# Split key and value weights made in the first attention, query stacks taken from DRAM, three key stages, one row product a unit, values multiplied by single key tiles

## The reference, cut to what matters

```
q = layernorm(x) @ Wq.T + bq ; k = ctx @ Wk.T + bk ; v = ctx @ Wv.T + bv
scores = q . k / sqrt(32)          (L1: clipped to +-50, masked keys at -50)
heads = softmax(scores) @ v ; x = x + tanh(gate) * (heads @ Wo.T + bo)
```

## Time and profile before

| | before |
|---|---|
| median of 3 executions | 3316.87 us |
| the profiled execution, its own time | 3318.72 us |
| its span on the core | 3316.8 us |
| mean granted TensorE clock | 0.894 of 2.4 GHz |
| busy share of the span: TensorE, VectorE, ScalarE, GpSimd | 81%, 57%, 36%, 30% |
| first attention, its blocks | about 0 to 330 us |
| L1 attention, start to the last take | about 545 to 971 us |
| L2 attention | about 1635 to 2090 us |
| L3 attention | about 2380 to 2840 us |

### The profile page before, as it was taken

One profiled execution on the slowest core, in us unless ns is written; L12 is line 12 of the kernel. 1 busy time (PEld: TensorE's weight loads), 2 busy tenths in 40 slices (PEclk: granted clock), 3 DMA queues, 4 the chain that ended last, 5 costly groups with the idle time before them and its releaser, 6 DMA issues. The chain is left out here.

```text
span 3316.8 us, 36567 instructions
## 1 busy us (share of the span) xinstructions
PE 2702.4 (81%) x11319; PEld 1708.5 (52%) x11319; DVE 1898.5 (57%) x3303; ACT 1208.7 (36%) x2586; POOL 984.4 (30%) x438
## 2 busy tenths in 40 slices
PE   7998797787787289999678888748678888789898
PEld 3554686544323156566365553336455553367565
DVE  3453675487665898985647774512347774534321
ACT  2111222355543597874114444211214444212111
POOL 2000000366713011010017776033217776032122
PEclk9988898878888599999788998879888998899999
DMA  9520122232200101010223221073423321021722
GB/s 325 163 75 22 70 76 101 76 111 63 77 1 29 38 14 51 26 51 13 87 61 106 76 52 36 1 255 73 136 62 101 80 54 36 14 92 48 261 55 47
DMA packets 122048, 258.08 MB, mean 78 GB/s; under 512 B 26656, under 2 KB 29729, under 8 KB 118561
## 3 DMA queue, kind: packets, MB, share of 16 engines
q1 hardware_dynamic: 104672, 218.70, 21.1%
q0 software_dynamic: 12864, 29.06, 3.7%
q10 hardware_dynamic: 4352, 8.39, 0.8%
HBM read 155.44 MB, written 47.39 MB: 61 GB/s over the span
## 5 line engine op out<-in xcount | busy, mean ns | idle before, releaser
L1768 POOL TENSOR_TENSOR L_attn_total<-L_attn_total,L_attn_probs 128x2048 f32<-128x2048 f32 x120 | 554.1, 4618 | 145.7 <-ACT L_attn_probs L1707 139.5
L1707 ACT ACTIVATE L_attn_probs<-L_attn_s_ps 128x512 f32<-128x512 f32 x512 | 290.6, 597 | 373.3 <-PE L_attn_s_ps L1588 366.1
L1813 DVE TENSOR_REDUCE L_attn_row_max<-L_attn_rows_ps 128x1 f32<-128x512 f32 x512 | 336.7, 682 | 151.3 <-PE L_attn_rows_ps L1568 146.1
L1588 PE MATMUL L_attn_s_ps<-L_attn_q_stack,L_attn_k_stack 98*128 98x512 f32 (+1 forms) x768 | 334.7, 468 | 106.9 <-ACT L_attn_probs L1707 76.7
L516 PE MATMUL L_ffn_hidden<-L_ffn_x_high,L_ffn_up_high 128*128 128x512 f32 x688 | 296.1, 430 | 100.6 <-DVE L_ffn_routes L432 53.4
L398 ACT ACTIVATE L_ffn_sums<-sims 128x128 f32<-128x128 f32 x1024 | 315.4, 390 | 46.8 <-DVE L_ffn_routes L418 26.4
L1588 PEld LDWEIGHTS L_attn_s_ps<-L_attn_q_stack,L_attn_k_stack 98*128 98x128 f32 (+1 forms) x768 | 154.6, 208 | 262.6 <-ACT L_attn_probs L1707 119.1
L516 PE MATMUL L_ffn_hidden<-L_ffn_x_low,L_ffn_up_high 128*128 128x512 f32 x688 | 272.9, 397 | 0.0
L1568 PE MATMUL L_attn_rows_ps<-L_attn_k_stack,L_attn_q_stack 96*128 96x512 f32 x512 | 217.4, 448 | 45.3 <-DVE L_attn_row_max L1813 43.0
L537 PE MATMUL L_ffn_y<-L_ffn_down_in,L_ffn_h 128*128 128x512 f32 x512 | 230.8, 596 | 2.0 <-DVE L_ffn_h L644 2.0
L1707 ACT ACTIVATE L_attn_probs<-L_attn_s_ps,keep_mask 128x512 f32<-128x512 f32 x256 | 182.9, 781 | 126.5 <-DVE L_attn_s_ps L1825 126.2
(11 more groups left out here) (297 smaller groups left out, 4700.6 us busy)
## 6 DMA issues: line engine op xcount, KB each, us to landing
L_attn_ctx<-ctx_parts SPq DMA_DIRECT2D x12, 2048.0 KB, 10.7
L_attn_k_stack<-L_attn_kh SPq DMA_DIRECT2D x384, 64.0 KB, 2.0
L_attn_abs_in<-in_L_ffn_w SPq DMA_DIRECT2D x12, 1024.0 KB, 10.0
L_attn_q_stack<-L_attn_qh SPq DMA_DIRECT2D x192, 64.0 KB, 2.0
L_attn_k_stack<-L_attn_kl SPq DMA_DIRECT2D x192, 64.0 KB, 2.0
L_ffn_x_slots<-L_attn_blank SPq DMA_DIRECT2D x46, 258.5 KB, 14.5
L_ffn_xg<-L_ffn_x_slots POOLq DMA_DIRECT2D x46, 258.5 KB, 4.8
L_ffn_up_all<-in_L_ffn_w SPq DMA_DIRECT2D x16, 704.0 KB, 13.8
```

The costliest lines, as they stand in the source:

```text
L1588: nc.tensor.matmul(s_ps[:, v % S_SLOTS, :], k_stack[0:depth, n % 2, h, kt * P:(kt + 1) * P], q_stack[0:depth, n % Q_SLOTS, h, :], start=Tr ...
L1707: nc.scalar.activation(probs[:, g % P_SLOTS, h, :], s_ps[:, v % S_SLOTS, :], ACT.Exp, **kinds).then_inc(exp_done, 1)
L1768: nc.gpsimd.tensor_tensor(total[:], first, probs[:, g % P_SLOTS], ALU.add).then_inc(added, 1)
L1813: nc.vector.tensor_reduce(row_max[:, hq, i:i + 1], rows_ps[:, r % R_SLOTS, :], AX_X, ALU.max, negate=True).then_inc(max_done, 1)
```

## The change: what it does

1. The key and value weights of L1, L2 and L3 are split once, in the loop of the first attention: round f loads one group of one layer (128 x 1024) into later_raw, ScalarE casts it, GpSimd subtracts, and ScalarE's queue stores both parts in DRAM (kv_parts). The two parts share the slots of the context pieces, so the waits for the context stores move ahead of the loop. The attentions load the parts straight into wk and wv, which have one buffer each, and split nothing.
2. Queries are split straight from PSUM, stored in DRAM (q_parts) and stacked by three DMAs a set.
3. Keys and queries go through three stages instead of one kh/kl and one qh/ql. Each stack has semaphores of its own.
4. Row products come one a unit, the first eight a set earlier, at units 24 to 31; join moves to unit 24 and turn to 26.
5. Items alternate V, K, V, K; pv takes one key tile in every fourth unit. On SyncE the fold comes last, behind the weight and context loads.

```diff
+        self.wk, self.wv = sb("wk", [P, 2, DC * P], F32R), sb("wv", [P, 2, 2, DC * P], F32R)
...
-    SUMS_AT, TURN_AT, COPY_AT, PV_AT, PV_EVERY = 7, 27, 5, 2, 8
-    LAST_ROW = 25
-    QUERY_HIGH_AT, QUERY_LOW_AT = 9, 10
+    SUMS_AT, TURN_AT, COPY_AT, PV_AT, PV_EVERY = 7, 26, 5, 2, 4
+    JOIN_AT, EARLY_ROWS = 24, 8
+    STAGES = 3
...
-        return ("V", n // 2 + 1, n % 2 * 2 + number) if number < 2 else ("K", n + AHEAD, number - 2)
+        return ("K", n + AHEAD, number // 2) if number % 2 else ("V", n // 2 + 1, n % 2 * 2 + number // 2)
...
+        if u >= JOIN_AT:
+            return [(n + 2, u - JOIN_AT)] if n + 2 < SETS else []
+        if n + 1 == SETS:
+            return []
+        if n:
+            return [(n + 1, EARLY_ROWS + u)]
+        first = 5
+        return [(1, r) for r in range(max(u - first, 0) * ROWS // (JOIN_AT - first),
+                                      max(u - first + 1, 0) * ROWS // (JOIN_AT - first))]
...
+                def store_queries(b, f):
+                    sp.wait_ge(product_free, place["Q", b, f] + 1)
+                    sp.dma_start(env.q_parts[b * FG + f].bitcast(F32),
...
                 def stack_queries(n):
-                    sp.wait_ge(query_low, n + 1)
+                    sp.wait_ge(query_stored[n], 16)
...
-                    for h in range(HG):
-                        for r, part in enumerate((qh, qh, ql)):
+                    for r, part in enumerate((0, 0, 1)):
...
+                def next_key_weights(n):
+                    sp.wait_ge(product_done, place["K", n - 1, KH - 1] + 1)
+                    parts.load_key_weights(env, sp, n % FG)
+
+                def next_value_weights(pair):
+                    sp.wait_ge(product_done, place["V", pair - 1, V_ITEMS - 1] + 1)
+                    parts.load_value_weights(env, sp, pair % (FG // PAIR))
+
+                store_queries(0, 0)
                 stack_queries(0)
+                for f in range(1, FG):
+                    store_queries(0, f)
                 stack_keys(0, 0)
                 stack_keys(0, 1)
+                next_key_weights(1)
                 stack_queries(1)
+                next_value_weights(1)
+                for f in range(FG):
+                    store_queries(1, f)
                 if less_max_rows:
                     fold(0)
                 stack_keys(1, 0)
                 stack_keys(1, 1)
+                next_key_weights(2)
                 for n in range(SETS):
                     if n and n + 1 < SETS:
                         stack_keys(n + 1, 1)
                     if n + AHEAD < SETS:
                         stack_queries(n + AHEAD)
                         stack_keys(n + AHEAD, 0)
                     if n == FG - AHEAD - 1:
                         sp.wait_ge(product_done, place["K", FG - 1, 0] + 1)
                         parts.load_context(env, sp, 1, 0)
-                    if less_max_rows and n + 1 < SETS:
-                        fold(n + 1)
+                    if n % 2 and n // 2 + 2 < SETS // PAIR:
+                        next_value_weights(n // 2 + 2)
+                    if n + AHEAD + 1 < SETS:
+                        next_key_weights(n + AHEAD + 1)
                     if n == FG - AHEAD - 1:
                         sp.wait_ge(product_done, place["K", FG - 1, 1] + 1)
                         parts.load_context(env, sp, 1, 1)
+                    if less_max_rows and n + 1 < SETS:
+                        fold(n + 1)
...
                         if u % PV_EVERY == PV_AT:
-                            g = KT * n + u // HG - 2
-                            for kt in range(max(g, 0), g + 2):
-                                pv(kt)
+                            g = KT * n + u // HG - 1
+                            if g >= 0:
+                                pv(g)
...
+                def high_part(item):
+                    act.wait_ge(product_done, place[item] + 1)
+                    at = split_count[item] - 1
+                    if at >= STAGES:
...
+                    nc.scalar.activation(stage[:, stage_of[item], 0, :], bank(item), ACT.Identity, bias=bias_of(item)).then_inc(
+                        split_high, 1)
...
+                def low_part(item):
+                    dve.wait_ge(split_high, split_count[item])
+                    nc.vector.scalar_tensor_tensor(stage[:, stage_of[item], 1, :], bank(item), bias_of(item),
...
+                def load_later(f, m):
+                    act.wait_ge(later_low, LATER * f + m + 1)
...
+                def split_later(f, m):
+                    act.wait_ge(later_loaded, 16 * (LATER * f + m + 1))
+                    act.wait_ge(later_stored, 16 * (LATER * f + m) + 1)
+                    nc.scalar.copy(later_part[:, :, 0, :], later_raw[:]).then_inc(later_high, 1)
+
+                def store_later(f, m):
+                    act.wait_ge(later_low, LATER * f + m + 2)
...
+                for n in range(PART_SLOTS):
+                    act.wait_ge(part_stored[n], 16 * len(range(n, PIECES, PART_SLOTS)))
                 with act.Fori(0, FG) as f:
...
                     for i in range(PRODUCTS):
+                        if i % 4 == 0:
+                            load_later(f, i // 4)
+                        elif i % 4 == 2:
+                            split_later(f, i // 4)
...
+                        if i % 4 == 3:
+                            store_later(f, i // 4)
...
+                with pool.Fori(0, FG) as f:
+                    for m in range(LATER):
+                        pool.wait_ge(later_high, LATER * f + m + 1)
+                        nc.gpsimd.tensor_tensor(later_part[:, :, 1, :], later_raw[:], later_part[:, :, 0, :].bitcast(F32),
+                                                ALU.subtract).then_inc(later_low, 1)
```

289 lines of the change are left out of this document (116 added, 173 removed).

## The result

The changed kernel took **3201.05 us** at the median of four executions (3195.44 to 3213.95), the kernel before 3317.57. The ratio is 0.9655, with a 95% interval of 0.9624 to 0.9686. Forecast were 3143 us and a range of 3075 to 3225: the sign and the range held, but a third of the gain did not come. The profiled execution took 3213.95 us, the slowest of the four, with a span of 3212.3 us at a mean granted clock of 0.91 (0.894 before).

What follows compares the result with a forecast made beforehand. Hand-overs, not work per unit, were taken as the bound: VectorE's splits, ScalarE's kh, L2's set end, the clock. L1 -62.9, L2 and L3 -123.8, first attention +13 sum to -173.7: 3145.0 profiled, so 3143 us; range 3075 to 3225.

Steps and rivals of the forecast that it cites:

- B: Rival: GpSimd's loop and half clock stay, each wait for an add a thin stretch of falling clock; 3207 us, chance 0.18.
- step 4: L2, sets 1 to 5, join(1) to join(6): 240.4 us to become 5 x 38.5 = 192.5, -47.9.
- Step 1: L1, sets 1 to 4, take(0) to take(4): 185.0 us to become 149.2, -35.8, removing ScalarE waits and splits.
- Step 6: L2, prologue and set 0: gain as in L1's prologue, with rows in it; -10, between 0 and -18.
- step 3: L1, prologue and set 0: waits go, but TensorE stands about 11 us at unit 8; -18, between -8 and -25.
- Step 1 and 2: L1's sets: -35.8 for sets 1 to 4, -8.6 for sets 5 and 6, -2 for the last set.
- Step 5: L2's end, join(6) to last take: GpSimd's adds of set 6 start two to three units earlier; -12, between -3 and -20.
- Step 7: Set 1's context loads: the fold on SyncE stands behind other loads; +8 in L2, +1.5 in L1.
- Step 8: First attention: TensorE stands about 8 us for context stores, plus low clock and late splits; +13, between +3 and +30.
- The weighed rule: First attention: GpSimd and VectorE lock each other out; twelve subtracts could cost 30 us in all, giving 3173 us.
- C: Rival: loads on ScalarE's queue become the bound in the first attention; slower, about 3377 us, chance 0.02.
- D: Rival: items still meet a busy bank or stage, so sets gain only some 80 us; 3238 us, chance 0.05.

Runs made afterwards that it cites:

- the extra operations: Changed kernel with an empty VectorE difference of two constant 128x512 tensors at nine places a layer where the earlier kernel split weights: 3269.6 us, ratio 0.9836.
- the old rows: Changed kernel with row products back at units 1 to 25 of the set before, join at unit 26 and turn at 27: 3223.0 us, ratio 0.9705.

## Why the prediction was right or wrong, step by step

**The shortfall.** Against the profiled execution 69 us are missing from my sum: 29 in L1, 14 in each of L2 and L3, 2 in the first attention, 10 in blocks that the change leaves alone. Nearly all terms are off to one side, so the range held by its width: it was made to take in B.

**Right.** The mechanism of step 4: no splits on VectorE, one row a unit and an early fold bring L2's set to 38.9 us (38.5 forecast) at full clock. Between join(1) and join(6) the extra operations give back 24.1 us, the old rows 9.8 (215.8 against 206.0), and one stage in place of three, with V, V, K, K in both, 7.1 (224.3 against 217.2). These are 41 us against a gain of 34.5, but that gain is net: the single tiles took 7.3 us from it (198.7 with two) and the fold behind the context loads 9.2 (196.8 with the fold ahead). So some 51 us were gained, and about 10 of them no run assigns; as the edits were run apart, they need not add.

In L1 the gain came in the main from ScalarE's freed wait and not from VectorE's splits: V, V, K, K with one stage gives back 19.8 of the 30.5 us from take(0) to take(5), the extra operations at most the 4 us by which these runs differ. Step 1 took this wait as 4.6 us in each set; in the five sets before the change there were three of them, 11.7 us in all. ScalarE's own share of the splits, casts of 0.61 us, was put back by no run.

Step 6 was right in size (-11.1 and -11.5 for -10; about -9 in L2 if it is read from the first exponential of set 1, which the moved join does not touch), and step 3 named the stand at unit 8 of set 0 and its size (about 11 us; 10.2).

**Step 1 and 2, the way back to GpSimd's next add.** I gave it 3.8 us a set in L1 with the clip, from mean durations (my own terms, 2.5 and 0.74, add to 3.2; the other 0.6 had no source); it is 5.9. Five sets of it are 10 of the 13 us that these two steps lack. I counted each operation once and left out that the chain breaks again at the second and third add. In L2, where TensorE is the bound, the same kind of omission is the 0.31 us of each visit to the value products: of the 1.8 us that single tiles cost I had 1 us, the take, and gave it no second part. The last set's +5.5 is in part this execution: it took 35.1 us here and 32.0 to 32.2 in seven of the edited kernels, against 29.6 before and 29.6 with two tiles a visit, where I had the single tile as a gain of 2.

**Step 3.** The gain of -18 was -9.7: the query stores behind the value weights (4.8 us on TensorE, with the clock behind it) were missing. That they alone make up the 8 us is not shown. I had followed the key stacks along SyncE's queue but not the stores that the change adds to it, which step 9 costed at nothing.

**Step 5, the end of L2 and L3.** -12 forecast, -2.1 and -2.3 measured. I let GpSimd's adds of set 6 start two to three units earlier. They do not: the first of them began 9.8 us behind the set's first exponential before and begins 8.9 us behind it now, and the last one ended 51.9 us after join(6) before, now 51.0. I also measured from join(6) and left out that the change moves it: from the first exponential of set 6 to the last take L2's end took 75.6 us before and 70.6 now, so 5.0 us were gained, and 3.0 of the missing 10 are the moved mark. GpSimd is at its floor there:

```profile
1955.14 4.68 POOL L1759 TENSOR_TENSOR L_attn_total<-L_attn_probs 128x2048 f32<-128x2048 f32 x1 [2.26 <-ACT L_attn_probs L1707]
1959.97 9.32 POOL L1759 TENSOR_TENSOR L_attn_total<-L_attn_total,L_attn_probs 128x2048 f32<-128x2048 f32 x2
1970.50 18.66 POOL L1759 TENSOR_TENSOR L_attn_total<-L_attn_total,L_attn_probs 128x2048 f32<-128x2048 f32 x4
```

34.0 us from first add to last with no gap but the normalise. TensorE, which has no items in set 6, gets there in 33.8 us and then stands 5.5 us, where in the last set of the kernel before it stood 3.5. The work for the last set after the sums takes about as long as ever: from the end of the last add to the last take 28.8 us before, 27.6 now.

**Step 7.** +8 a layer, +12 measured (50.6 against 38.9). The stand was 9.2 us, half way between 0 and my end of 18 (all 5.5 MB); the run with the fold ahead shows that the loads ahead are the cause. I had the mechanism and took too low a value because the nearest row was of one context load, not of everything ahead.

**Step 8.** +15.1 for +13, by two errors that partly cancel, and by luck: the issue of 5.6 us was missing, and the splits at i = 10 cost 0.1 us a round and not 0.8. The store wait was 8.2 us for my 8 in this execution. In the ten others with the same first attention the time to the first tile was 564.4 to 571.7 us, so the step costs 15 to 22 us, and 13 lies below all of them.

**The weighed rule.** GpSimd's twelve subtracts of 2.35 us cost nothing in the first attention, as the rows said, but they did not put the rule to the test: none of them met a piece of VectorE's row quantisation, which runs at 80, 147, 200 and 252 us for 4 to 5 us each. The one piece that met a GpSimd operation, a subtract of the context pieces, took 1.36 us instead of 0.48 (1.52 before the change). What VectorE does beside the twelve subtracts, small operations on PSUM (0.483 us for the most frequent) and four sums over one tensor in SBUF (2.28 us), took as long as before. The Trainium skill (SBUF — State Buffer, section SBUF: two separate sides) has VectorE and GpSimd lock each other out for an operation with two SBUF inputs; the extra operations agree, 4.08 against 0.68 us. The low part of a key item, which reads PSUM and one tensor in SBUF, took 0.75 us beside GpSimd's operations and away from them.

**The rivals.** B's number, 3207, is the nearest to 3201, but its mechanism did not come in L2, where the clock does not fall in a full set. Only L1 looks like B, with clocks of 0.84 to 1.00 in sets 1 to 4. C and D did not come.

**All else, +10.5 us**, lies in blocks that the change leaves alone. From L2's last take to L3's first query product this execution took 317.8 us; the kernel before 310.4, the twelve edited kernels 309.2 to 315.3. It is the spread of these blocks, and a part of why the profiled execution is the slowest of four.
